# The sums behind the network's second products, 28 recurrence steps later, in a fused decoder kernel

## What is computed

```python
def step(carry, u):                       # one position, 64 real and 64 imaginary states per batch
    sr, si = sr * decay + r * 0.1, si * decay + i * 0.1
    nr = clip(sr * c - si * s, -10, 10)
    ni = clip(sr * s + si * c, -10, 10)
h = einsum(spectral_out, W_from)
x2 = x + h * 0.1
h = gelu(layernorm(x2) @ W_ffn1.T + b1)   # 256 -> 1024
h = h @ W_ffn2.T + b2                     # 1024 -> 256
x = layernorm(x + (x2 + h * 0.1))
x = layernorm(x + cross_attention(x, ctx))    # 16 heads
```

## Time and profile before

| | |
|---|---|
| median of three runs (lowest, highest) | 2190.64 us (2190.49, 2192.05) |
| the profiled execution's own time | 2187.26 us |
| its span | 2185.5 us |
| mean granted TensorE clock | 0.898 of full speed |
| busy share: PE / VectorE / ScalarE / GpSimd | 81% / 67% / 48% / 22% |
| blocks 1 to 7 of the recurrence with what runs beside them | 120.5 to 609.0 us of the span |
| from there to the barrier | 609.0 to 701.4 us |

### The profile page before, as it was taken

The page is one execution under the profiler, slowest core; times in us unless marked ns, Lnnn a source line. Parts: engine busy times, 40 slices in busy tenths (PEclk is TensorE's granted clock), DMA queues, the critical chain, the costliest instruction groups (busy, mean ns, idle before and its releaser), DMA issues.

```text
span 2185.5 us, 34752 instructions
## 1 busy us (share of the span) xinstructions
PE 1770.1 (81%) x12793; PEld 1280.6 (59%) x12793; DVE 1460.3 (67%) x4900; ACT 1040.8 (48%) x2545; POOL 486.0 (22%) x554
## 2 busy tenths in 40 slices
PE   3555667666776887899999999999888999998808
PEld 1344556555665344566666766666657999884306
DVE  4887767777733488676777567777735666663695
ACT  3534445544543753455555345555314455543762
POOL 3011101110110012333333333333302333330002
PEclk9666888778996996899999999999989999999959
DMA  5000000000000010100000000000303333310001
GB/s 153 1 1 1 1 1 1 1 1 1 2 1 1 0 39 20 63 1 1 1 1 1 1 1 1 1 1 1 125 4 88 88 84 67 85 30 0 0 0 39
DMA packets 86315, 49.83 MB, mean 23 GB/s; under 512 B 40205, under 2 KB 83905, under 8 KB 85953
## 3 DMA queue, kind: packets, MB, share of 16 engines
q1 hardware_dynamic: 79361, 47.05, 8.3%
q10 hardware_dynamic: 6784, 0.56, 0.3%
HBM read 45.50 MB, written 2.10 MB: 22 GB/s over the span
## 4 chain that ended last, share of the span: by engine, by line
PE 60%; DVE 17%; ACT 11%; issue 3%; POOL 2%; POOLq 0%; DVEq 0%; ACTq 0%
PE PS L1587 6%; PE PS L1614 6%; PE PS L1885 6%; PE PS L1601 5%; PE PS L1572 3%; PE PS L1562 3%; PE PS L2298 3%; PE PS L1948 2%; PE PS L763 2%; PE PS L769 2%; PE PS L1629 2%; DVE sq L712 2%; DVE nx L709 2%; PE PS L937 2%; PE PS L1904 2%
## 5 line engine op out<-in xcount | busy, mean ns | idle before, releaser
L1741 POOL TENSOR_SCALAR px<-px,crl 128x128 f32<-128x128 f32 (+7 forms) x128 | 225.9, 1765 | 419.0 <-DVE crl L1713 419.0
L1652 ACT ACTIVATE px<-PS,cnm 128x128 f32<-128x128 f32 (+7 forms) x256 | 189.3, 740 | 264.9 <-DVE cnm L1698 258.0
L709 DVE TENSOR_TENSOR_SCAN nx<-sq 128x6 f32<-128x6 f32 x1024 | 184.8, 180 | 37.2 <-SPq L2365 2.3
L712 DVE TENSOR_SCALAR sq<-nx 128x4 f32<-128x4 f32 x1024 | 186.2, 182 | 35.0
L1695 DVE TENSOR_REDUCE cm<-PS 128x1 f32<-128x128 f32 (+6 forms) x224 | 154.2, 688 | 55.4 <-PE PS L1587 54.9
L1601 PE MATMUL PS<-ident,px 128*128 128x128 f32 x1152 | 157.8, 277 | 13.2 <-ACT qT L1640 9.5
L1601 PEld LDWEIGHTS PS<-ident,px 128*128 128x128 f32 x1152 | 129.1, 141 | 60.3 <-issue 34.8
L1587 PE MATMUL PS<-kT,qT 64*128 64x512 f32 (+3 forms) x768 | 158.3, 517 | 4.5 <-ACT px L1652 2.6
L1614 PEld LDWEIGHTS PS<-pT,V 128*64 128x64 f32 x2304 | 124.1, 137 | 63.5 <-issue 34.5
L1614 PE MATMUL PS<-pT,V 128*64 128x128 f32 x2304 | 154.1, 278 | 6.4 <-DVE pT L1706 2.8
L192 POOL TENSOR_SCALAR rstd<-mv 128x1 f32<-128x1 f32 x88 | 32.4, 369 | 563.9 <-DVE mv L171 563.9
(11 more groups left out here) (332 smaller groups left out, 3933.0 us busy)
## 6 DMA issues: line engine op xcount, KB each, us to landing
xbs<-in_fside_Bx16xSxS SPq DMA_DIRECT2D x8, 1232.0 KB, 6.6
fsrc<-in_fside_Bx16xSxS SPq DMA_DIRECT2D x8, 1232.0 KB, 6.6
xmk<-in_mask_Bx16xSxS_bk SPq DMA_DIRECT2D x8, 308.0 KB, 8.3
fsrc<-in_mask_Bx16xSxS_bk SPq DMA_DIRECT2D x8, 308.0 KB, 8.3
X<-in_x SPq DMA_DIRECT2D x1, 2048.0 KB, 11.9
w<-in_L_attn_W_ffn SPq DMA_DIRECT2D x2, 1024.0 KB, 11.9
t<-in_L_ffn_w SPq DMA_DIRECT2D x2, 1024.0 KB, 11.4
out<-xs SPq DMA_DIRECT2D x16, 128.0 KB, 1.7
```

The source lines that it names most:

```text
L709: e.tensor_tensor_scan(k.nx[:, :], d0, d1, 0.0, ALU.mult, ALU.add).then_inc(sem("rec.scan"), 1)
L712: e.tensor_scalar(o, bass.AP(k.nx, 2, [[6, P], [0, 2], [3, 2]]), 10.0, -10.0, ALU.min, ALU.max).then_inc(sem("rec.clip"), 1)
L1652: e.activation(k.px[n % 2][:, h, 0:width], src, ACT.Exp, scale=-1.0, bias=k.cnm[:, n % 4, h:h + 1], accum_out=k.cl[:, n % 4, h:h + 1]).the ...
L1741: e.tensor_scalar(k.px[n % 2][:, 0, 0:width], k.px[n % 2][:, 0, 0:width], k.crl[:, n % 4, 0:1], None, ALU.mult).then_inc(sem("c.normal0"), 1)
```

## The change

Two gaps of the network's chain. The second `down` product is placed 8 instead of 6 recurrence steps behind the first. The first `sum` of the norm behind it is placed 28 instead of 10 steps behind that product for tile pairs 0 to 5, and 14 steps for pair 6; for pair 7, which has no recurrence beside it, the gaps have no effect. No instruction is added or taken away.

```diff
     yield 3, ("down", 0, t)
-    yield 6, ("down", 1, t)
-    yield from norm(2, 10)
+    yield 8, ("down", 1, t)
+    yield from norm(2, 28 if t < BT - 2 else 14)
```

## The result

The changed kernel takes 2215.86 us, the median of four runs (2214.47 to 2216.02), against 2190.56 for the kernel before beside it: a ratio of 1.0114, with an interval of 1.0096 to 1.0131. It is 25 us slower; 2211.2 was predicted, in a range of 2194 to 2229. The span of the profiled execution is 2213.9 us at a clock of 0.892, 28.4 more than the 2185.5 at 0.898 of before.

A forecast was written before the change was run, and what follows sets the result against it. In-order VectorE was taken as the bound, its waits stopping the recurrence. Block 1 -2.3, blocks 2 to 6 +7.5, block 7 +8.1 and behind the recurrence +7.3 gave +20.6, so 2211.2 us, range 2194 to 2229.

The forecast's parts named there:

- the 6.9 us of `normal`: VectorE's wait for TensorE's spread in blocks 2 to 6; claimed to go, with 1.0 to 2.5 us to spare.
- a wait of 10.6 us for the score: VectorE, second tile's second maxima, blocks 2 to 6: claimed to replace a wait of 2.3 to 3.3 us.
- The first crossing: ScalarE, blocks 2 to 6: exponentials and query copies now precede shift; first up at 27.4 us instead of 21.5.
- the second: TensorE, blocks 2 to 6: the score now behind eight up, mix, down and spread, before behind three up; maxima at 45.9 us.
- GpSimd's additions, which now fall there, some 0.4: Between first and second maxima of a block: additions claimed to cost VectorE 0.4 us, second maxima starting at 12.3.
- block 7: Last block of the recurrence: score behind mix and both down, claimed to take 77.4 us, +8.1.
- clock regained: Rival, TensorE: all eight up at 2.4 GHz, sum +4.4 us; chance 0.10 together with the no-effect rival.
- Clock lost: Rival, TensorE: 1.2 GHz through all eight up, 26 us more, 2237; chance 0.08.
- Behind the recurrence: From the recurrence's end to the barrier: a scores round moves here, down at 42.8 us against 35.5, +7.3.
- Faster: Rival, blocks 2 to 6: the normal wait goes and nothing replaces it, about -13 us, 2178; chance 0.12.
- No effect: Rival, whole kernel: engines wait for semaphores, so the delay may vanish, 2190.6 us; chance 0.10 together with clock regained.
- the estimated +5 us: ScalarE table loads: by the page's 2.66 us, 0.9 us a block more, about +5 in all; left out of the forecast.

The follow-up runs named there:

- r10: Changed kernel with the first norm's shift, side and turn put ahead of the first tile's maxima and exponentials, second down kept in place: 2194.45 us, 1.0028.
- r4: Changed kernel with the second tile's first maxima and following score eight places earlier, ahead of the first down and spread: 2196.83 us, 1.0045.
- r6: Changed kernel with GpSimd's three kinds of additions done on one column instead of 256: 2194.41 us, 1.0022.

## Why the prediction was right, and where it was off

**Right: the wait is exchanged for a longer one.** The prediction had the 6.9 us of `normal` going and a wait of 10.6 us for the score in its place, with 1.3 before it. The trace has 9.57 and 2.47, none of `normal`, and one table load pair a block instead of two (ten fewer ScalarE instructions in all). The first crossing (ScalarE meets the exponentials and query copies before `shift`) and the second (the score stands behind all `up`) are both shown to carry most of the loss, by r10 and by r4.

**Off: the step to the second maxima.** From the hand-over of block 3, with the places predicted:

| | predicted | measured |
|---|---|---|
| first maxima | 7.2 | 7.8 |
| second maxima | 12.3 | 14.7 |
| first `up` | 27.4 | 30.2 |
| second tile's second maxima | 45.9 | 47.9 |
| end of the block | 73.5 | 74.9 |

The term that failed is "GpSimd's additions, which now fall there, some 0.4". All five fall there, five operations of VectorE take 0.65 instead of 0.17 us, and that is 2.4. Without the additions (r6) the second maxima of block 3 start at 11.9 and the first `up` at 27.1. Another 0.6 is lost ahead of the first maxima, where the bias of line 1113, pushed over the edge of the block, stands behind the hand-over copies. I had read the additions as lying beneath a reduction, as one of them does in the kernel before; the walk of the list had `out` at place 75 and did not ask what a place two or three steps past the block's last one does. The sums from there on were good: maxima to `up` 15.4 against 15.1, `up` to the second tile's maxima 17.7 against 18.5 (whose terms, as listed, add up to 18.6 to 18.8), the rest 27.0 against 27.6. The net of 1.6 us a block makes the 8 us by which blocks 2 to 6 miss.

**Off the other way: block 7.** Forecast 77.4, measured 75.0. The first `up` came when predicted, 27.3 us after the hand-over, and after 2.29 us of idle time on TensorE, but all of them ran at the full clock: 1.00 from 581.1 on, as the last row of the windows above shows. Eight `up` and the score took 8.3 us and not 11.1. The step that was wrong is that the clock of block 3 was carried over to block 7. Nothing was regained there: over the `up` of block 7 the kernel before had the full clock already.

```profile
560.00:568.50 8.50, 7.76 (x42) 6.16 (x40) 4.09 (x16) 5.08 (x9) 0.00 (x0) 1.00 0.00 0
```

In block 3 the clock was 0.90 over the stretch of the `up` and `down` (283.1 to 300.8), so the start ran low, as I took it, though for 3.4 us and not for 5.3: the 24-record score at 284.53 took 1.93 us against 1.07 in block 7. So the rival *clock regained* did not come: the one block that has the full clock had it before. *Clock lost* did not come: `down(0)` at 295.65 took the 3.72 us of before.

**Behind the recurrence.** +7.3 was predicted, +8.5 measured. The mechanism is the one given: `from` no longer queues, and a whole round of scores has moved here. `peak(14)` stands at 30.4 against a forecast of 28.5, `down` at 44.7 against 42.8.

**The other rivals.** *Faster* needed the first `up` ahead of the exponentials; it was 30 us after the hand-over. It names the right lever all the same: in r10 the first norm's `shift` to `put` come ahead of the exponentials, the first `up` comes right behind these and the query products at 26.2, and most of the loss is gone. *No effect* falls with the ratio. The table loads: after each the first GELU starts at once or behind its product (282.94 + 1.28 is 284.22, and the GELU at 284.64 waited 0.42 for TensorE), so no drain shows here either, and the estimated +5 us worked out from the drain that the Trainium skill's page "ScalarE: Activation LUTs", section "What ACT_TABLE_LOAD costs", states stays unseen.

**The size came out closer than its parts.** 4.7 us lie between forecast and median. Blocks 2 to 6 were 8.0 too low and block 7 was 2.3 too high, and the rest of the ledger came within 2. Against the profile the sum is 20.6 to 28.4; the medians differ by 25.3 only, since the profiled execution of the kernel before was 3.3 us faster than its median. That block 7 and this difference lean against the miss of blocks 2 to 6 is luck.

## What to carry over

When all engines walk one list, moving one step moves everything that is chained to it, and a wait that disappears is replaced by whatever the moved steps now cross on the in-order engines: walk the list engine by engine and ask of each step what long work stands ahead of it now. In this kernel it paid to move the consumer that waits (`normal`, by 16 places, 30 us gained) and not the producer chain that others hang on (25 us lost). Side work that slows another engine was free only where a wait behind it absorbed it, so price it by the place in which it lands, above all where a step slips over the edge of a block.

## What was not expected of the hardware

The same additions of GpSimd (0.70 us each) slow the two operations of the recurrence from 0.17 to 0.65 us, and not the reductions from PSUM beside them: in the kernel before, one of 2.27 us ran over an addition of 0.72, no longer than any other. The Trainium skill's page "SBUF — State Buffer", section "SBUF: two separate sides", says that VectorE and GpSimd take a shared pair of ports as an exclusive lock for a whole instruction, in some forms of VectorE's operations only. The trace agrees as far as it goes: 0.65 is about the length of one addition, the scan with its two inputs in SBUF is held, and the reduction from PSUM is not. The clip of line 712 has one input in SBUF and is held as well; no run here shows which of the page's forms it takes.

That block 7's `up` started at 2.4 GHz after 2.29 us of idle time, while those of blocks 2 to 6 ran their first products at 1.2 GHz after only 1.69 us, was not expected either, and stays open. In the kernel after, the granted clock was 0.50 from 355.4 to 362.0, with the first `up` of block 4 at 358.24, and from 283.7 to 287.0, just behind the first `up` of block 3 at 283.07. The idle time just ahead is not what decides it: with the score moved (r4), the same 2.29 us in block 7 are followed by 0.50 from 560.5 to 563.7. Block 7's TensorE work before it is otherwise placed (its `from` products ran 0.59 us each, block 3's 1.06), and no run varied that alone.
